# Two attention blocks and a mixture of experts on one core: small DVE, ACT and POOL jobs put elsewhere in a hand-written order

## The reference

```
x   = L0_attn_x
xn  = layernorm(x)
out = x + attention(xn) + ffn(xn)
ffn: x1 = xn + rotary_attention(rmsnorm(xn)) @ wo;  xf = rmsnorm(x1)
     probs = softmax(xf @ gate_w.T);  sel = top_k(probs + bias_e, 4)
     rw = probs[sel] / max(sum(probs[sel]), 1e-12)
     ffn = x1 + sum_e cw[e] * (silu(xf @ weg) * (xf @ weu)) @ wed + shared(xf)
```

## Time and profile before

| | |
|---|---|
| median of 3 runs | 782.0 us (779.44 to 782.55) |
| profiled execution | 780.95 us, its span 779.2 us |
| PE busy | 740.5 us, 95% of the span |
| DVE, ACT, POOL busy | 578.4, 513.2, 490.5 us |
| DMA | 76.99 MB, mean 99 GB/s |
| granted TensorE clock | full but for the stretch from about 430 to 460 us |

### The profile page before, as it was taken

One profiled execution on the slowest core, in us unless ns is written; L12 is line 12 of the kernel. 1 busy time (PEld: TensorE's weight loads), 2 busy tenths in 40 slices (PEclk: granted clock), 3 DMA queues, 4 the chain that ended last, 5 costly groups with the idle time before them and its releaser, 6 DMA issues.

```text
span 779.2 us, 14673 instructions
## 1 busy us (share of the span) xinstructions
PE 740.5 (95%) x4700; PEld 662.1 (85%) x4700; DVE 578.4 (74%) x1732; ACT 513.2 (66%) x1270; POOL 490.5 (63%) x563
## 2 busy tenths in 40 slices
PE   7899999999999999999998469999999999999997
PEld 4688888898888898889877358999999999999996
DVE  7898979788887977667885146776667767677775
ACT  5777778777787765675445145677666766667663
POOL 6766769677777784344677712466647766676564
PEclk9999999999999999999999679999999999999999
DMA  6000000000100299101014360067795777767734
GB/s 192 22 14 21 14 22 16 26 15 15 55 29 28 83 311 268 38 15 42 15 34 98 107 190 1 29 155 169 186 248 137 183 166 172 173 153 153 159 38 162
DMA packets 102725, 76.99 MB, mean 99 GB/s; under 512 B 6951, under 2 KB 101499, under 8 KB 102651
## 3 DMA queue, kind: packets, MB, share of 16 engines
q1 hardware_dynamic: 91890, 63.41, 28.7%
q0 software_dynamic: 10608, 12.61, 10.5%
q10 hardware_dynamic: 152, 0.06, 0.0%
HBM read 51.36 MB, written 24.69 MB: 98 GB/s over the span
## 4 chain that ended last, share of the span: by engine, by line
PE 67%; DVE 12%; ACT 11%; issue 4%; another core or an unknown queue 3%; DMA 2%; POOL 1%; SPq 0%; DVEq 0%; POOLq 0%; ACTq 0%
PE j L937 18%; PE zb L937 11%; PE ob L937 10%; PE s L937 9%; PE t L1093 6%; ACT probs L1279 3%; PE j L1041 2%; DVE probsT L1607 2%; DVE probs L1592 2%; PE ob L1041 2%; DMA moe_sum_dram<-late,slot_tokens 2%; PE zb L1041 1%; ACT probsT L1294 1%; ACT rope_swapped L1319 1%
## 5 line engine op out<-in xcount | busy, mean ns | idle before, releaser
L735 POOL TENSOR_SCALAR probs<-probs,inv_sum 128x256 f32<-128x256 f32 (+1 forms) x239 | 142.2, 611 | 144.4 <-DVE inv_sum L1598 139.6
L1279 ACT ACTIVATE probs<-probs,neg_max 128x128 f32<-128x128 f32 (+3 forms) x256 | 143.5, 561 | 105.3 <-DVE neg_max L1592 85.3
L937 PE MATMUL s<-k_heads,q_heads 128*128 128x256 f32 (+2 forms) x576 | 139.0, 362 | 8.2 <-DVE neg_max L1592 7.7
L1592 DVE CUSTOM_DVE_ANT_0 probs<-s,mask 128x128 f32<-128x128 f32 (+3 forms) x256 | 119.9, 485 | 14.3 <-PE s L937 10.4
L823 POOL DMA_INDIRECT moe_sum_dram<-late,slot_tokens x63 | 103.0, 1635 | 26.3 <-ACT late L1367 13.2
L1607 DVE TENSOR_TENSOR probsT<-t,probsT 128x384 fp32r<-128x384 f32 (+2 forms) x192 | 101.5, 549 | 22.1 <-ACT probsT L1294 18.0
L1093 PE MATMUL t<-ident,probs 128*128 128x128 f32 x640 | 95.6, 276 | 12.7 <-issue 10.7
L1294 ACT ACTIVATE probsT<-t 128x384 fp32r<-128x384 f32 (+2 forms) x192 | 90.1, 488 | 25.9 <-PE t L1093 15.2
L937 PEld LDWEIGHTS s<-k_heads,q_heads 128*128 128x128 f32 x576 | 91.6, 191 | 15.2 <-DVE neg_max L1592 11.6
L1093 PEld LDWEIGHTS t<-ident,probs 128*128 128x128 f32 x640 | 74.3, 142 | 19.4 <-issue 11.6
L937 PE MATMUL zb<-probsT,v_heads 128*128 128x512 f32 (+2 forms) x351 | 69.4, 342 | 2.3 <-DVE xnT L1651 1.3
(11 more groups left out here) (291 smaller groups left out, 1665.1 us busy)
## 6 DMA issues: line engine op xcount, KB each, us to landing
x_slots_dram<-mask SPq DMA_DIRECT2D x1, 8480.0 KB, 39.2
late<-x_slots_dram SPq DMA_DIRECT2D x32, 265.0 KB
late<-in_L_ffn_weg_dram SPq DMA_DIRECT2D x63, 128.0 KB
late<-in_L_ffn_weu_dram SPq DMA_DIRECT2D x63, 128.0 KB
late<-in_L_ffn_wed_dram SPq DMA_DIRECT2D x63, 128.0 KB
moe_sum_dram<-mask SPq DMA_DIRECT2D x2, 1152.0 KB, 7.1
raw_qk<-in_L_ffn_wq_dram SPq DMA_DIRECT2D x16, 128.0 KB, 2.4
raw_o<-in_L_ffn_wo_dram SPq DMA_DIRECT2D x8, 256.0 KB, 2.7
```

What stands on the lines that cost most here:

```text
L735: pool.tensor_scalar(piece, piece, rinv[:, u % 2, i:i + 1], 1.0, ALU.mult, ALU.mult).then_inc(p_norm, 1)
L937: m = pe.matmul(dst, lhs(a), rhs(b), start=first and i == 0, stop=last_ and i == 2, skip_group_check=skip)
L1279: act.activation(piece, piece, ACT.Exp, bias=nmax[:, u % 2, i:i + 1], scale=-1.0, accum_out=rsum[:, u % 2, i:i + 1]).then_inc(e_done, 1)
L1592: ve.tensor_tensor_reduce(pr[:, u % 2, P_OFF[i]:P_OFF[i] + width], bS[i % 2][:, 0:width], mask_t[:, S - width:S], INV_SCALE, BIG, ALU.add, ...
```

## The change

Eight edits, all in the order or place of existing work but for the weight sums:

1. DVE, rotary steps with n = 1 mod 4: the query's cosine product stands ahead of the inverse of tile 3.
2. DVE, rotary steps with n = 2 mod 4: the mask of tile 3 stands behind `probs_lo` of group 2 and the blocks over from the step before.
3. POOL: the split of the second output-weight pair of groups 1, 2 and 3 stands in steps 9, 17 and 25 instead of 10, 18 and 26.
4. POOL: its wait for the rope table stands behind three weight splits, at the first product that reads the table.
5. ACT: squares and scaled rows of steps 31 to 34 stand behind the copies of the turned groups; the four rows of the first batch entry are scaled in step 34, between the copy of group 2 and the exp of tile 2.
6. DVE: the ranks (comparison, sum, copy and two shifted additions) move from the end of step 38 to step 39, behind the masks of tiles 0 and 1; the sums of the choice weights, the division by their sum and the copy of slot numbers move there from POOL, as two sums, a maximum, a reciprocal, a product and a copy. POOL's `sum_choice` goes, with its semaphore and a constant.
7. The waits for `rows_done` count one signal, DVE's, instead of three.
8. PE, last unit: group 2 is turned into bank s1 and first, ahead of the out projections, and waits for the last mask instead of for bank t0 or t1.

```
-    SCALED = {(HALF + 1, 1): (0, 1), (HALF + 2, 1): (2, 3), (HALF + 3, 0): (4, 5), (HALF + 3, 1): (6, 7)}
+    SCALED = {(HALF + 2, 0): (0, 1, 2, 3), (HALF + 3, 0): (4, 5), (HALF + 3, 1): (6, 7)}
...
-        if s == 2:
+        if s == (1 if 0 < a < HALF // GS else 2):
             found.append(("O1", a))
...
+        def turn_bank(u, c):
+            return bS[1] if (u, c) == (UNITS - 1, 2) else bT[(3 * u + c) % 2]
...
-            sp.wait_ge(rows_done, 3)
+            sp.wait_ge(rows_done, 1)
             expert_weights(SHARED + 1)
...
                 if k == 0:
-                    pool.wait_ge(rows_done, 3)
+                    pool.wait_ge(rows_done, 1)
...
-            def sum_choice(n):
-                if n == RANKS:
-                    weights = x2r[:, :, D + 1 + TOPK:ROW]
-                    pool.wait_ge(weighed, 1)
...
                     if n == -2 and job[0] == "Q3":
+                        pool.wait_ge(rope_in, 16)
                         q_sin(n, it)
...
-            pool.wait_ge(rope_in, 16)
             windows(pool, step)
...
-                until(pe, pt_lo, at + 1, it, 3 * GS)
+                if (u, c) == (UNITS - 1, 2):
+                    pe.wait_ge(s_free, TB * UNITS + 2)
+                else:
+                    until(pe, pt_lo, at + 1, it, 3 * GS)
...
             def last_unit():
+                turn_probs(UNITS - 1, 2, None)
                 for t in range(2):
                     out_project(UNITS, t, None, (0,))
-                turn_probs(UNITS - 1, 2, None)
...
                     z_part(n, it)
-                    if n in SQUARED:
-                        kept(act, ("O", FINAL[SQUARED[n][0]]))
-                        squares(SQUARED[n])
-                    scale_rows(SCALED.get((n, 1), ()))
                     guests(n, 5)
                     if nxt:
                         probs_hi(n + 1, 0, it)
                     guests(n, 6)
                     if nxt:
                         probs_hi(n + 1, 1, it)
+                    if n in SQUARED:
+                        kept(act, ("O", FINAL[SQUARED[n][0]]))
+                        squares(SQUARED[n])
+                    scale_rows(SCALED.get((n, 1), ()))
...
-                if v_last or k_last:
+                if v_last:
                     mask_scores(n + 1, 3, it)
                 probs_lo(n, 2, it)
                 for ch in over_from(n):
                     chunk(ch, it)
-                if not v_last and not k_last:
+                if not v_last:
                     mask_scores(n + 1, 3, it)
...
                 invert(n + 1, 2, it)
-                if v_last:
+                if k_product or v_last:
                     chunk(chs[0], it)
                 for ch in k_last:
                     rope_sum(ch, it)
                 invert(n + 1, 3, it)
-                if k_product:
-                    chunk(chs[0], it)
                 rope_sum(chs[0], it)
...
                 if n == RANKS + 1:
+                    then(ve.tensor_tensor(over_b, count_e.unsqueeze(2).to_broadcast([P, E, 8]),
+                                          thr_t[:, :].unsqueeze(1).to_broadcast([P, E, 8]), ALU.is_gt))
+                    then(ve.tensor_reduce(blocks_e, over_b, AX.X, ALU.add))
+                    then(ve.tensor_copy(run[0][:, E:2 * E], blocks_e))
+                    ve.wait_ge(ones_done, 4)
+                    shift_add(1)
+                    shift_add(2)
+                    ve.wait_ge(weighed, 1)
+                    weights = x2r[:, :, D + 1 + TOPK:ROW]
+                    then(ve.tensor_reduce(weights, match, AX.X, ALU.add))
+                    then(ve.tensor_reduce(rsm[:, 3], weights, AX.X, ALU.add))
+                    then(ve.tensor_scalar(rsm[:, 0], rsm[:, 3], 1e-12, None, ALU.max))
+                    then(ve.reciprocal(rsm[:, 1], rsm[:, 0]))
+                    then(ve.tensor_tensor(weights, weights, rsm[:, 1].unsqueeze(2).to_broadcast([P, NT, TOPK]), ALU.mult))
+                    then(ve.tensor_copy(x2r[:, :, D], slot_t[:, 1:1 + NT]))
                     for s in (4, 8, 16):
                         shift_add(s)
```

More of the change, by code:

```diff
@@ L874, in step @@
                 name_choice(n)
-                sum_choice(n)
                 if n == -1:
@@ L1981, in route_1 @@
                     match_out(range(4, NT))
-                if n == RANKS:
-                    then(ve.tensor_tensor(over_b, count_e.unsqueeze(2).to_broadcast([P, E, 8]),
-                                          thr_t[:, :].unsqueeze(1).to_broadcast([P, E, 8]), ALU.is_gt))
-                    then(ve.tensor_reduce(blocks_e, over_b, AX.X, ALU.add))
-                    then(ve.tensor_copy(run[0][:, E:2 * E], blocks_e))
-                    ve.wait_ge(ones_done, 4)
-                    shift_add(1)
-                    shift_add(2)
                 if n == RANKS + 1:
```

30 lines of the change are left out of this document (4 added, 26 removed).

## The result

The changed kernel takes 786.39 us, the kernel before 782.36 (medians of 22 runs each): ratio 1.0047, 95% interval 1.0036 to 1.0059. It is slower by 4 us where 3.15 less were forecast. Two later comparisons gave 1.0035 (1.0022 to 1.0048) and 1.0035 (1.0015 to 1.0056). The profiled execution took 786.62 us, span 784.8, so 5.6 us over the span of before.

What follows compares the result with a forecast made beforehand. It took the kernel as a TensorE matmul stream (95% busy) with a few waits for softmax links. Terms -3.45 + 1.3 - 0.4 - 1.1 + 0.9 - 0.4 = -3.15 us gave 778.8 us, range 770.5 to 785.

Steps and rivals of the forecast that it cites:

- the hole: 427 to 454 us, units 41 and 42: signals reach ACT late during POOL's scatters, costing some 27 us; nothing removes it.
- rival E: Units 41 and 42: the hole grows as more late signals fall into the scatters; 789 us, chance 0.10.
- The cosine product: Units n = 1 mod 4: rotary sum 0.7 us sooner, about 0.6 a pair; with the mask move, 3.45 us less.
- the port rule: Two-SBUF-input DVE and SBUF-reading GpSimd instructions exclude each other; by it the split could cost +2.2, not +1.3.
- The split: Units 9, 17, 25: turn of 10 and 18 1.1 us later, mask waits in 11 and 19 gone; +1.3 us.
- Squares and scaled rows: Units 31 to 35: moved behind the turned blocks, they give PE 1.1 us back.
- Unit 39: Ranks and weight sums there delay v and all after it by 0.9 us, 1.4 gained included: +0.9.
- the last unit: Third turned block goes to a free score bank and is turned at once; attend 0.4 us sooner.
- The rope wait: Start of kernel: POOL's first weight split no longer waits for the rope table; 0.4 us less.
- B: Stream closes everywhere: port collisions go, the split costs nothing, unit 39 breaks even; 774 us, chance 0.15.
- C: Units 41 and 42: the hole shrinks, two fewer signals caught by the scatters; 767 us, chance 0.10.
- D: DVE carries unit 39: contended block costs 2.2 us, the split 2.4 with nothing back; 781.3 us, chance 0.20.

Runs made afterwards that it cites:

- c0: The changed kernel itself, run again beside the kernel before on another chip: ratio 1.0035, median 759.26 us.
- g0: The changed kernel run once more, as the one to compare g1 with on the same chip: ratio 1.0035, median 782.86 us.
- d1: c3 with DVE's output-projection addition put ahead of the rotary sum in units 5, 9, 13, 17, 21, 25: ratio 0.9921, 774.56 us.
- c3: c2 with unit 1's cosine product alone back behind the last inverse: ratio 0.9921, median 750.39 us.
- d2: c3 with the mask of tile 3 put back ahead of the turned block's low part: ratio 0.9921, median 774.91 us.
- d4: c3 with the cosine product back behind the last inverse in the other units too: ratio 0.9968, median 778.75 us.
- a2: The changed kernel with only the output-weight split put back one unit later (10, 18, 26): ratio 0.9976, median 753.54 us.
- d3: c3 with the output-weight split one unit earlier, as in the changed kernel: ratio 1.0027, median 782.96 us.
- a3: The changed kernel with ranks and weight sums put back where they were: ratio 1.0023, median 757.66 us.
- c2: The changed kernel with the output-weight split back, scaled rows 6 and 7 earlier, ranks and weight sums back: ratio 0.9945, median 752.72 us.
- a1: The changed kernel with only the squares and scaled rows put back ahead of the turned blocks: ratio 1.0044, median 759.06 us.
- g1: The changed kernel with unit 36's router matmuls cut in three, score tiles 2 and 3 between them: ratio 1.0053, median 784.80 us.

## Why the prediction was wrong

It was wrong in the sign. At full clock, and without what loads and the hole scatter, the units of the changed kernel sum to 2.0 us more, not 3.15 less (0.75 - 0.75 - 0.24 + 2.43 - 1.46 + 0.74 + 0.95 - 0.44); by the mean clocks, drops add 0.8 us in c0 and 1.7 in g0; in the first comparison, where the clocks of before are not on record for each execution, 2.0 of the 4.0 us are left to drops and the hole. The time is nearest to that of rival E, 789, but not by E's cause.

**The cosine product: the step that failed.** "PE gets back the 0.25 before the score and, as the mask at 152.89 comes 0.6 sooner, the 0.4 behind it: about 0.6 us a pair of units" gave -3.45; the pairs named there, with 1-2 and 5-6, came to -0.24. The 0.25 and the 0.4 did come back (0.26 ahead of unit 14's first score, 0.41 up to its turn), and nearly all of it was lost again at two turns. In unit 13 the rotary sum that comes 0.7 sooner lands on POOL's normalisation of tile 3 and stretches it by 0.5 us (1.0 in unit 1): PE's turn and what follows lose 0.29. In unit 14 POOL's last normalisation ends no sooner than before, and PE, there 0.4 too early, loses 0.32. So the stretch is one half, which d1 and c3 show, and the link behind it the other: without the stretch d1 gains 0.13 a pair. No order of the two DVE edits that was run makes the plain pairs more than 0.1 us shorter than before (17.65; c3 17.57, d2 17.64, d4 17.55). The prediction took the gain to its end without asking what stands next at the turns. It used the port rule for the split and not here; its lower bound of 0 had the copies as the cause, and none reached below 0, where unit 1 was (+1.0).

**The split: mechanism right, size off.** The turn of units 10 and 18 came 1.35 us later, counted from the start of unit 9, against 1.1: 1.98 for the split, 1.07 given by the earlier q, and 0.44 of stretch in the normalisations. Units 11 and 19 did become 0.3 shorter each, but not by the split: they are so in a2 too, where the split is back, and 8.23 us again in d4, where the cosine product is. The prediction's reading of the stretched row was wrong. DVE's 1.53 us at 193.04 began beside POOL's low part of q and not beside the split, which came a microsecond later; in a2 the same DVE instruction takes 0.68 us and has ended before the split begins, and it is POOL's low part beside it that is stretched (1.57). Net +2.43 for both places against +1.3. What this hid: without it the new order gives 1.1 and 0.8 there (a2: 25.5 us for 9 to 11 against 26.6 before, and for 17 to 19 against 26.3), so its own price is 4.3 us, a2 and d3 alike. "The pair's own gain is swallowed" was put at 0.6. By the port rule the give-back was to be nil because the split would meet another DVE sum; in unit 9 it met none (0.62 and 1.28 us).

```profile
193.02 1.01 POOL L838 TENSOR_TENSOR q_heads<-rope_sum,q_heads 128x384 fp32r<-128x384 f32 x1
```

```profile
122.83 0.68 DVE L1649 TENSOR_TENSOR k_heads<-rope_sum,k_heads 128x512 fp32r<-128x512 f32 x1
```

The first is POOL before, the second DVE in a2, whose split starts at 124.35.

**Squares and scaled rows: half seen.** -1.46 against -1.1 in 33 to 35. The row at the end of unit 35 was not followed to its reader: PE turns rows 4 to 7 one unit on, and waits, +0.74.

**Unit 39 and the last unit: right.** The block took 1.54 + 1.22 + 1.07 us for ranks, sum and small operations (1.6, 1.2, 1.1 forecast); v came 0.95 late (0.9), and a3 and c2 take exactly that back. The last unit gave -0.44 against -0.4, though no run undid its edit alone.

**The rope wait: not seen.** The first score stands at 17.5 to 18.6 us over all traces, a scatter in which 0.4 is lost; no run undid that edit alone. The waits of units 50 to 56 scatter as much: unit 50 takes 16.5 to 18.4 us.

**The clock: not in the prediction.** It took the drops for a part of the hole. Two idle times of 2.3 us can bring new ones, worth 1.6 us for each 3.4 us.

**The rivals.** B falls: POOL had no room. C and E fall: the hole follows the chip or the session and not the order, and beside a hole of 23 to 27 us no edit is seen, only a scatter. D had the right place, POOL beside DVE, but in unit 39, where POOL's sums were gone and nothing was stretched. Its price for the split, 2.4 with nothing back, meets the measured 2.43 by other terms.

## What to carry to other kernels

When an instruction is moved forward, look at what runs on the other engine at its new time, and at what it pulls forward with it: here a sum moved 0.7 us onto a neighbour's instruction gave back nearly half of what was won, and the next link in line took most of the rest. A gain counts only up to the next link that stands there. A job put ahead of a queue without idle time costs its full length plus what the queue's users lose, and a wait of PE costs more than its length where it lowers the clock. Follow each moved result to its reader, one unit on too. Here one edit of eight cost more than the rest gave: with it back, the rows earlier, the ranks and unit 1 as before, the ratio is 0.992 instead of 1.0035.

## What the runs showed of the hardware

- A POOL multiplication by a column, 128x512, takes 0.70 us beside a DVE instruction with one SBUF input (before and d1, unit 13), 1.19 to 1.20 beside one with two (c3, after), and 1.71 beside two of them in a row (after, unit 1).
- The hole of 23 to 27 us beside POOL's 32 scatters is there on two of four chips, and in the first comparison, and absent on the two others, with the same scatters at the same pace.
- One 3.4 us drop of TensorE's clock to its lower level costs 1.6 us; behind an idle time of 2.3 us it came at once in two traces (a1, g1), and units later or not at all in others. In d3 and d4 it came in unit 36 with no idle time of PE ahead of it in that unit.
